# Moving a head's 512 negated maxima through a row in memory instead of eight transfers of 128

## The chip, the cores and the metric

The kernel runs on one core of one Trainium2 chip. The metric is the device time of one execution in microseconds (us). Before the change the median of three runs is 3677.85 us (3670.58, 3677.85 and 3678.45).

## The reference

A "macaron" layer on 4096 tokens of width 256 in float32: half a feed-forward layer, attention, half a feed-forward layer again, each behind a layer norm.

```python
x = x + 0.5 * ffn(layernorm(x))
x = x + attn(layernorm(x))
x = x + 0.5 * ffn(layernorm(x))
# attn: 16 heads of 16 channels
ctx = X @ We.T                                    # 32 channels
influence = einsum('bqe,bke->bqk', ctx, ctx)      # the same for all heads
scores = einsum('bhqd,bhkd->bhqk', Q, K) / 4 + 0.1 * influence[:, None]
attn = softmax(scores); out = (attn @ V) merged @ Wo.T
# ffn: both operands of each product are rounded to 4-bit floats in blocks of 16
```

The change lies in the attention: every query of every head needs the maximum of its 4096 scores, negated, before the exponentials.

## The kernel before, in words

**Stages.** A weights phase, a first feed-forward phase, a projection phase (q, k, v and ctx, parked in DRAM scratch), the attention, an output phase, and a second feed-forward phase. The attention takes 64 steps (STEPS). A step handles two heads (HEADS) and one block of 512 queries (QB, eight blocks to a pair of heads) against all 4096 keys.

**Two passes over the scores.** A coarse product (L1360) multiplies 128 queries by 512 keys into one of three PSUM banks, and VectorE (L1537) reduces the bank to its maximum per query in `tops`. A step has 64 such units, 32 to a head. They run ahead: in step s the coarse units 16 to 63 belong to step s+1, and units 0 to 15 to step s+2. After unit 32 VectorE folds head 0's 32 partial maxima into `neg_max` (L1551, 128 partitions x 4 columns: query j*128+p lies on partition p in column j); after the first unit of step s+2 it does so for head 1. The fine product (L1394) computes the scores transposed, 128 keys by 512 queries, in several accumulating products. ScalarE takes the exponential (L1522) into a ring of probabilities, and TensorE multiplies them by the values (L1404) into `o_ps`. A step has eight groups (NG); a group has eight coarse units, eight fine tiles and their products with the values, in an order written out by hand (SEGMENTS).

**How the maximum enters.** `queries.low[head][n]` holds, in each half of the partitions (rows r*64 on), the 32 rows of low parts of the queries, then at row 32 (M_ROW) the 512 negated maxima, then 16 more rows. The keys hold ones in that row, so the fine product subtracts the maximum. Both halves need the same row. Head 0's tile enters fine products named "low", and negated by GpSimd (`negate`, L1242) "old"; head 1's enters "new" (in the trace `fine<-area,key_d`). The tiles are double buffered over steps.

**SyncE's queue in step s.** SyncE issues nearly all transfers, in program order: wait until step s-1's exponentials are done (L1298); `load_low` for s+1, 8 transfers (L807, L809); `load_cross`, 2 (L801); `load_coarse` for s+2, 8 (L794, L795); `load_max(s+1, 0)`, 8 (L1280); then for the results of step s-1 `copy_sum` (2, L1125), `save_inverse` (1 to DRAM, L1130), `spread_inverse` (2 back, L1136) and `store` (2, L1143); in five of eight steps two transfers of the next pair's keys (L1263, L1265, L1272); last `load_max(s+1, 1)`, 8 (L1280).

**Who waits for what.** GpSimd, in order: `add_halves` for step s-1, `negate(s+1)` (needs head 0's maxima loaded, L1240), `multiply` for step s-1 (needs `spread_inverse`). VectorE inverts the sums at unit 50 (`INVERT_AFTER`, L1155), for which `copy_sum` must have landed. TensorE waits for `m_loaded` of head 0 and of head 1 only in group 0 of the step that uses them (L1457, L1462). Before it writes `neg_max[n]` again, two steps later, VectorE waits that the transfers that read it have ended (L1550).

Of the kernel before, what the change touches and what calls it, by code (L numbers as in the profile page):

```python
# [23 lines left out]
F32 = mybir.dt.float32  # L24
# [6 lines left out]
P = 128  # L31
T = 4096
TT = T // P
D = 256
# [3 lines left out]
DE = D // 8  # L38
# [5 lines left out]
QB = 512  # L44
NQB = T // QB
KT = T // P
QT = QB // P
KB = T // 512
HEADS = 2
STEPS = H // HEADS * NQB  # L50
# [703 lines left out]
HALF = P // 2  # L754


def half_rows(r, first, count):

    return slice(r * HALF + first, r * HALF + first + count)
# [339 lines left out]
M_ROW = 2 * DK  # L1099
# [63 lines left out]
def attention_phase(nc, sem, ident, v_all, scratch, sums, first_keys, probs, reload, first, area, second_low, parts, w):  # L1163

    with ExitStack() as ctx:
# [4 lines left out]
        queries = first.queries  # L1170
        tops = [sb(f"tops{n}", [P, HEADS * QT, KB]) for n in range(2)]
        neg_max = [sb(f"neg_max{n}", [P, HEADS * QT], F32R) for n in range(2)]
# [17 lines left out]
        k_loaded, low_keys_loaded = [[sem(f"{name}_loaded{n}") for n in range(2)] for name in ("k", "low_keys")]  # L1190
        m_loaded = [[sem(f"m_loaded{head}_{n}") for n in range(2)] for head in range(HEADS)]
        late_v, late_copied, part_ready = sem("late_v"), sem("late_copied"), sem("part_ready")
        table_loaded, negated = sem("table_loaded"), sem("negated")
        fine_ready, probs_ready, pv_done = sem("fine_ready"), sem("probs_ready"), sem("pv_done")
        coarse_ready, tops_ready, neg_ready = sem("coarse_ready"), sem("tops_ready"), sem("neg_ready")

        TILES = 2 * HEADS * PAIRS
        P_LEAD, V_LEAD = 2 * TILES_IN_GROUP, 4
        C_DMAS, K_DMAS, LOW_KEYS_DMAS, M_DMAS = [16 * 4, 16 * 2], 16 * 2, 16 * 8, 16 * 2 * QT
        LATE = KEPT * QT // 2  # L1200
        LATE_BLOCKS = sorted(range(NQB - KEPT, NQB), key=lambda b: b % KEPT < IN_AT)
        V_AFTER = [2 * i + 1 for i in range(LATE)]
# [21 lines left out]
        with nc.Block() as block:  # L1224
# [32 lines left out]
            def _(sp):  # L1257
# [16 lines left out]
                def load_max(s, head):  # L1274
                    n = s % 2
                    sp.wait_ge(neg_ready, HEADS * s + head + 1)
                    with nc.allow_non_contiguous_dma(reason="the maxima lie one to a partition"):
                        for r in range(2):
                            for j in range(QT):
                                sp.dma_start(queries.low[head][n][half_rows(r, M_ROW, 1), j * P:(j + 1) * P].bitcast(F32),  # L1280
                                             neg_max[n][:, head * QT + j:head * QT + j + 1].bitcast(F32)).then_inc(m_loaded[head][n], 16)

                for j in range(PIECES - 2, PIECES):
                    for r in range(2):
# [8 lines left out]
                for head in range(HEADS):  # L1293
                    load_max(0, head)

                def step(s):
# [10 lines left out]
                    if s + 1 < STEPS:  # L1307
                        load_max(s + 1, 0)
# [16 lines left out]
                    if s + 1 < STEPS:  # L1325
                        load_max(s + 1, 1)
# [337 lines left out]
def macaron_kernel(nc, x, wq, wk, wv, wo, we, w_gate, w_up, w_down, out):  # L1664
    with ExitStack() as ctx:
        sem = lambda name: ctx.enter_context(nc.semaphore(name))

        def sbufs(stack, shapes):
# [4 lines left out]
        ATTN_W = {f"{n}_{part}": ([P, KD, P if n == "e" else D], F32R) for n in "vqke" for part in ("hi", "lo")}  # L1673
        dram = {name: nc.dram_tensor("saved_" + name, shape, F32, kind="Internal").ap() for name, (shape, dt) in {**FFN_W, **OUT_W}.items()}
        scratch = {name: nc.dram_tensor("scratch_" + name, [rows, T], F32, kind="Internal").ap()
                   for name, rows in [("c_key", 2 * DE), ("c_query", 2 * DE)]} | {n: nc.dram_tensor("scratch_" + n, [D, 2, T], F32, kind="Internal").ap() for n in "qk"} | {"inv_sums": nc.dram_tensor("scratch_inv_sums", [STEPS, HEADS * QB], F32, kind="Internal").ap()}

        keep = sbufs(ctx, {"x_all": ([P, TT, D], F32), "ident": ([P, P], F32), "stats": ([P, TT, 6], F32),
                           "mean": ([P, TT], F32), "var": ([P, TT], F32), "tmp": ([P, TT], F32), "rstd": ([P, TT], F32), "root": ([P, TT], F32)})
# [23 lines left out]
        queries = Queries(sem, early_sb["slots"], [area[:, cols] for cols in SLOTS_IN_AREA], scratch)  # L1703
# [19 lines left out]
        second_low = both.enter_context(nc.sbuf_tensor("key_d0", [P, T // 2], F32R))  # L1723
        parts = [second_low[:, n * KD * QB:(n + 1) * KD * QB].rearrange("p (k t) -> p k t", k=KD) for n in range(2)]
        attention_phase(nc, sem, ident, v_all, scratch, sums, first_keys, probs, reload, first, area, second_low, parts, w)
        again.update({n: home[:, 0:KD * 2 * I].rearrange("p (a b) -> p a b", a=KD) for n, home in (("gu_hi", early_sb["slots"]), ("gu_lo", area))})
        output_phase(nc, sem, x_again, norm, again, parts, (o_reload, 16 * len(OUT_W)), (x_reload, 16 * X_PARTS), sums, [(again[n].bitcast(F32), dram[n], ffn_reload) for n in ("gu_hi", "gu_lo")])
# [20 lines left out]
```

## Time and profile before

| | us |
|---|---|
| median of three runs | 3677.85 |
| the profiled execution, its own time | 3675.19 |
| its span, first to last instruction | 3673.2 |
| PE busy | 3600.8 (98%) |
| DVE busy | 3165.5 (86%) |
| ACT busy | 2539.0 (69%) |
| POOL busy | 704.3 (19%) |
| DMA packets | 282101, 148.61 MB |

PE is TensorE's matmuls, PEld its weight loads, DVE VectorE, ACT ScalarE, POOL GpSimd, and SPq is SyncE's queue, where a row's duration is the time that issuing the transfer took. "Landing" is counted from the start of the issue. Times in a timeline are microseconds from the start of the span. Matmuls overlap in the pipeline, so a busy PE says little by itself: its waits are to be read at the weight loads, where an idle time stands in brackets with what ended it.

### The profile page before, as it was taken

How to read it: one execution, taken by the hardware profiler on the slowest of the kernel's cores; microseconds unless marked ns; L12 is line 12 of the kernel's file. 1: busy time of each engine (PE TensorE's matmuls, PEld its weight loads, DVE VectorE, ACT ScalarE, POOL GpSimd, SP SyncE). 2: the span in 40 equal slices, each digit the busy share in tenths (PEclk: the TensorE clock that was granted, in tenths of full speed). 3: DMA queues.
4: the chain of work that ended last, by engine and by line, in shares of the span. 5: the costliest groups of instructions: out<-in, count | busy, mean ns of one | idle time of the engine just before them, and what ended most of it. 6: DMA issues, size and time to landing. Idle time of an engine off the chain costs nothing. (4 is left out here: it accounts for less than half of the span.)

```text
span 3673.2 us, 71176 instructions
## 1 busy us (share of the span) xinstructions
PE 3600.8 (98%) x26663; PEld 2107.7 (57%) x26663; DVE 3165.5 (86%) x5176; ACT 2539.0 (69%) x4751; POOL 704.3 (19%) x509
## 2 busy tenths in 40 slices
PE   5998999999999999999999999999999999999999
PEld 4997655555555555555555555555555555554898
DVE  7996788888888888888888888888888888883898
ACT  4764277777777777777777777777777777777565
POOL 5991100000000000000000000000000000001697
PEclk9999999999999999999999999999999999999999
DMA  3003512111111111111111111111111111121100
GB/s 136 19 19 139 145 31 42 31 28 33 38 32 27 35 35 34 27 36 36 33 27 35 37 33 27 36 36 33 27 35 36 33 27 36 42 54 30 38 20 22
DMA packets 282101, 148.61 MB, mean 40 GB/s; under 512 B 181792, under 2 KB 233408, under 8 KB 280768
## 3 DMA queue, kind: packets, MB, share of 16 engines
q1 hardware_dynamic: 276976, 140.37, 16.1%
q10 hardware_dynamic: 4816, 4.10, 0.4%
q8 instruction: 197, 3.23, 0.4%
q14 instruction: 112, 0.92, 0.1%
HBM read 106.79 MB, written 32.51 MB: 38 GB/s over the span
## 5 line engine op out<-in xcount | busy, mean ns | idle before, releaser
L1537 DVE TENSOR_REDUCE tops<-coarse 128x1 f32<-128x512 f32 x4016 | 2547.0, 683 | 329.3 <-PE coarse L1360 273.6
L1522 ACT ACTIVATE x_all<-fine 128x512 f32<-128x512 f32 x4096 | 2115.0, 602 | 815.6 <-PE fine L1394 815.6
L1360 PE MATMUL coarse<-key_a,slots 48*128 48x512 f32 x4076 | 1292.1, 446 | 1.7 <-DVE tops L1542 1.2
L1404 PE MATMUL o_ps<-x_all,values 128*17 128x512 f32 x8192 | 1077.7, 598 | 0.6 <-ACT x_all L1522 0.6
L1360 PEld LDWEIGHTS coarse<-key_a,slots 48*128 48x128 f32 x4076 | 531.6, 184 | 909.9 <-DVE tops L1537 693.8
L1394 PE MATMUL fine<-slots,key_b 33*128 33x512 f32 (+1 forms) x3072 | 675.9, 394 | 0.0
L1394 PE MATMUL fine<-slots,key_a 48*128 48x512 f32 x2048 | 573.5, 420 | 0.0
L1394 PE MATMUL fine<-area,key_d 49*128 49x512 f32 x2048 | 563.6, 393 | 0.0
L1394 PE MATMUL fine<-slots,area 64*128 64x512 f32 x2048 | 409.1, 394 | 0.0
L1394 PEld LDWEIGHTS fine<-area,key_d 49*128 49x128 f32 x2048 | 368.3, 186 | 53.5
L1394 PEld LDWEIGHTS fine<-slots,key_b 33*128 33x128 f32 (+1 forms) x3072 | 340.6, 187 | 51.2 <-ACT x_all L1522 2.3
L1404 PEld LDWEIGHTS o_ps<-x_all,values 128*17 128x17 f32 x8192 | 135.8, 95 | 320.1 <-ACT x_all L1522 309.1
L1148 POOL COPY half<-ot 49x512 f32<-49x512 f32 x63 | 38.4, 609 | 1357.2 <-ACT ot L1483 1357.2
L1394 PE MATMUL fine<-area,key_b 49*128 49x512 f32 x1024 | 266.0, 395 | 0.0
L1394 PEld LDWEIGHTS fine<-slots,key_a 48*128 48x128 f32 x2048 | 246.6, 186 | 31.8 <-ACT x_all L1522 8.3
L1394 PEld LDWEIGHTS fine<-slots,area 64*128 64x128 f32 x2048 | 197.1, 186 | 42.5
L1160 POOL TENSOR_TENSOR wide<-total,wide 48x512 f32<-48x512 f32 x63 | 80.7, 1281 | 604.6 <-DMA wide<-scratch_inv_sums 604.6
L453 POOL TENSOR_TENSOR xn<-xn,step 128x960 f32<-128x960 f32 (+2 forms) x70 | 143.5, 2050 | 50.3 <-ACT step L619 49.4
L1394 PEld LDWEIGHTS fine<-area,key_b 49*128 49x128 f32 x1024 | 142.2, 186 | 14.9 <-ACT x_all L1522 9.2
L454 POOL TENSOR_TENSOR xn<-xn,step 128x960 f32<-128x960 f32 (+2 forms) x70 | 143.2, 2045 | 5.5
L631 ACT ACTIVATE sg<-g_ps 128x704 f32<-128x704 f32 x64 | 48.7, 761 | 126.5 <-PE g_ps L112 126.5
L459 POOL TENSOR_TENSOR dst<-xn,scale 128x960 f32<-128x960 f32 (+2 forms) x70 | 116.0, 1657 | 12.0 <-POOL xn L454 10.0
(232 smaller groups left out, 3177.7 us busy)
## 6 DMA issues: line engine op xcount, KB each, us to landing
slots<-scratch_c_query SPq DMA_DIRECT2D x256, 64.0 KB, 2.0
slots<-scratch_c_query SPq DMA_DIRECT2D x124, 128.0 KB, 2.9
slots<-scratch_q SPq DMA_DIRECT2D x384, 32.0 KB, 1.9
slots<-scratch_q SPq DMA_DIRECT2D x128, 64.0 KB, 1.9
area<-scratch_q SPq DMA_DIRECT2D x128, 64.0 KB, 2.0
slots<-neg_max SPq DMA_DIRECT2D x512, 0.5 KB, 2.0
area<-neg_max SPq DMA_DIRECT2D x512, 0.5 KB, 2.0
x_all<-in_L_attn_X SPq DMA_DIRECT2D x4, 1024.0 KB, 12.4
```

The source lines that it names most:

```text
L453: chain(pool.tensor_tensor(xn[n][:, cols], xn[n][:, cols], step[n][:, cols], ALU.add))
L454: chain(pool.tensor_tensor(xn[n][:, cols], xn[n][:, cols], step[n][:, cols], ALU.subtract))
L459: pool.tensor_tensor(blocks_of(dst[n][:, cols]), blocks_of(xn[n][:, cols]), spread(scale[n][:, lo:hi], hi - lo), ALU.mult).then_inc(q_read ...
L631: act.activation(sg[:, :], g_ps[:, 0:I], ACT.Silu).then_inc(sg_ready, 1)
L1148: eng.tensor_copy(self.half[:, :], self.ot[2 * 32:2 * 32 + self.BOTH, :]).then_inc(self.moved, 1)
L1160: eng.tensor_tensor(self.wide[:, :], self.total[0:32 + DK, :], self.wide[:, :], ALU.mult).then_inc(self.result_ready, 1)
L1360: return pe.matmul(bank, queries.coarse[head][t % queries.COARSE[head]][rows, q * P:(q + 1) * P], key_a[t // NQB % 2][rows, kb * 512:(kb + ...
L1394: return pe.matmul(fine[slot % 2][:, r, :], keys, query, start=what == "keys", stop=what in ("low", "new"), skip_group_check=what in PARTS[1])
L1404: last = pe.matmul(o_ps[32 * part:32 * part + DK + 1, :], v_all[:, head_of(s, head), kt, :], probs[:, ring(g, HEADS * head + which), r, :] ...
L1522: act.activation(probs[:, ring(g, slot), r, :], fine[slot % 2][:, r, :], ACT.Exp).then_inc(probs_ready, 1)
L1537: dve.tensor_reduce(tops[t % 2][:, head * QT + q, idx % KB:idx % KB + 1], coarse_bank(t, idx), AX.X, ALU.max).then_inc(tops_ready, 1)
```

## The change

The eight transfers of a head (two halves by four columns, each 128 elements of 4 B from 128 partitions to a part of a row) are replaced by one transfer of all 512 elements to a row of a new DRAM scratch tensor, in the order of the queries, a wait of SyncE for its landing, and one transfer from that row to both row halves. `m_loaded` now counts one transfer to a head.

```diff
-        table_loaded, negated = sem("table_loaded"), sem("negated")
+        table_loaded, negated, max_saved = sem("table_loaded"), sem("negated"), sem("max_saved")
...
-        C_DMAS, K_DMAS, LOW_KEYS_DMAS, M_DMAS = [16 * 4, 16 * 2], 16 * 2, 16 * 8, 16 * 2 * QT
+        C_DMAS, K_DMAS, LOW_KEYS_DMAS, M_DMAS = [16 * 4, 16 * 2], 16 * 2, 16 * 8, 16
...
                 def load_max(s, head):
                     n = s % 2
                     sp.wait_ge(neg_ready, HEADS * s + head + 1)
+                    row = scratch["maxima"][HEADS * n + head:HEADS * n + head + 1, :]
                     with nc.allow_non_contiguous_dma(reason="the maxima lie one to a partition"):
-                        for r in range(2):
-                            for j in range(QT):
-                                sp.dma_start(queries.low[head][n][half_rows(r, M_ROW, 1), j * P:(j + 1) * P].bitcast(F32),
-                                             neg_max[n][:, head * QT + j:head * QT + j + 1].bitcast(F32)).then_inc(m_loaded[head][n], 16)
+                        sp.dma_start(row.rearrange("a (j p) -> p (a j)", p=P), neg_max[n][:, head * QT:(head + 1) * QT].bitcast(F32)).then_inc(max_saved, 16)
+                    sp.wait_ge(max_saved, 16 * (HEADS * s + head + 1))
+                    sp.dma_start(queries.low[head][n][M_ROW:P:HALF, :].bitcast(F32), row.to_broadcast([2, QB])).then_inc(m_loaded[head][n], 16)
...
-                   ... | {"inv_sums": nc.dram_tensor("scratch_inv_sums", [STEPS, HEADS * QB], F32, kind="Internal").ap()}
+                   ... | {"inv_sums": nc.dram_tensor("scratch_inv_sums", [STEPS, HEADS * QB], F32, kind="Internal").ap(), "maxima": nc.dram_tensor("scratch_maxima", [2 * HEADS, QB], F32, kind="Internal").ap()}
```

## Rows read from the trace of the kernel before

**Rows 1.** Busy time by stretch: start:end, length, PE, PEld, DVE, ACT, POOL, PEclk, DMA, GB/s
```profile
452.00:3398.00 2946.00, 2944.59 (x22491) 1526.97 (x22492) 2562.82 (x4210) 2151.10 (x4166) 242.52 (x254) 1.00 0.16 34
```
**Rows 2.** Waits of PEld and DVE, 460 to 3390: us in total, times, longest
```profile
PEld coarse L1360 <- DVE tops L1537: 692.3, 814, 0.9
PEld o_ps L1404 <- ACT x_all L1522: 308.8, 994, 1.5
...
DVE few L1155 <- DMA few<-total: 19.5, 1, 19.5
```
**Rows 3.** Busy time by group of one step, columns as in rows 1
```profile
1654.15:1659.90 5.75, 5.75 (x46) 2.98 (x46) 5.06 (x9) 4.63 (x10) 1.88 (x2) 1.00 0.41 103
1659.90:1665.65 5.75, 5.75 (x46) 3.00 (x46) 5.15 (x10) 4.13 (x9) 0.00 (x0) 1.00 0.08 1
1688.65:1694.40 5.75, 5.75 (x46) 2.98 (x46) 5.08 (x9) 4.15 (x9) 0.00 (x0) 1.00 0.03 0
```
**Rows 4.** Timeline of ACT, the first exponentials of successive groups
```profile
1660.94 2.07 ACT L1522 ACTIVATE x_all<-fine 128x512 f32<-128x512 f32 x4 [0.93 <-PE fine L1394]
1666.68 2.07 ACT L1522 ACTIVATE x_all<-fine 128x512 f32<-128x512 f32 x4 [0.92 <-PE fine L1394]
...
1689.75 2.06 ACT L1522 ACTIVATE x_all<-fine 128x512 f32<-128x512 f32 x4 [0.91 <-PE fine L1394]
1695.49 2.06 ACT L1522 ACTIVATE x_all<-fine 128x512 f32<-128x512 f32 x4 [0.92 <-PE fine L1394]
```
**Rows 5.** Timeline of SyncE's queue in the same step: start, duration
```profile
1660.98 5.03 SPq L1280 DMA_DIRECT2D slots<-neg_max  x8
1666.05 1.23 SPq L1125 DMA_DIRECT2D few<-total  x2
1674.27 0.31 SPq L1130 DMA_DIRECT2D scratch_inv_sums<-few  x1
1675.65 0.77 SPq L1136 DMA_DIRECT2D wide<-scratch_inv_sums  x2
...
1684.06 5.81 SPq L1280 DMA_DIRECT2D area<-neg_max  x8
1694.59 0.31 SPq L807 DMA_DIRECT2D slots<-scratch_q  x1
```
**Rows 6.** Timeline of DVE in it
```profile
1673.92 0.33 DVE L1155 RECIPROCAL few<-few 32x32 f32<-32x32 f32 x1
```
**Rows 7.** Timeline of POOL in it
```profile
1667.58 0.62 POOL L1242 TENSOR_SCALAR area<-slots 113x512 fp32r<-113x512 f32 x1 [10.79 <-DMA slots<-neg_max]
```
**Rows 8.** Timeline of PE, the next step's first product with head 1's maxima
```profile
1697.83 0.62 PE L1394 MATMUL fine<-area,key_d 49*128 49x512 f32 x2
```
**Rows 9.** DMA issues: count, KB each, median us from issue to landing
```profile
slots<-neg_max SPq DMA_DIRECT2D x512, 0.5 KB, 2.0
...
wide<-scratch_inv_sums SPq DMA_DIRECT2D x128, 32.0 KB, 1.8
...
few<-total SPq DMA_DIRECT2D x128, 2.0 KB, 1.8
...
scratch_inv_sums<-few SPq DMA_DIRECT2D x64, 4.0 KB, 1.3
```
**Rows 10.** Tile key_d, 1640 to 1702: one issue's ns min/median/max, then landing
```profile
L1265 SPq DMA_DIRECT2D key_d<-scratch_k x2: 590/608/626, 1680.4 to 1681.0; - x2
...
DMA to landing us min/median/max: 3.9/4.1/4.4
```
**Rows 11.** Queue of the transfers, 1660.9 to 1666.2: packets, MB, share of 16 engines
```profile
q1 hardware_dynamic: 1008, 0.00, 10.2%
```
**Rows 12.** Timeline of POOL: one row to a step
```profile
1240.54 0.61 POOL L1148 COPY half<-ot 49x512 f32<-49x512 f32 x1 [21.68 <-ACT ot L1483]
...
1470.58 0.61 POOL L1148 COPY half<-ot 49x512 f32<-49x512 f32 x1 [21.70 <-ACT ot L1483]
...
1931.27 0.61 POOL L1148 COPY half<-ot 49x512 f32<-49x512 f32 x1 [21.75 <-ACT ot L1483]
```

More of the change, by code:

```diff
@@ L1675, in macaron_kernel @@
         scratch = {name: nc.dram_tensor("scratch_" + name, [rows, T], F32, kind="Internal").ap()
-                   for name, rows in [("c_key", 2 * DE), ("c_query", 2 * DE)]} | {n: nc.dram_tensor("scratch_" + n, [D, 2, T], F32, kind="Internal").ap() for n in "qk"} | {"inv_sums": nc.dram_tensor("scratch_inv_sums", [STEPS, HEADS * QB], F32, kind="Internal").ap()}
+                   for name, rows in [("c_key", 2 * DE), ("c_query", 2 * DE)]} | {n: nc.dram_tensor("scratch_" + n, [D, 2, T], F32, kind="Internal").ap() for n in "qk"} | {"inv_sums": nc.dram_tensor("scratch_inv_sums", [STEPS, HEADS * QB], F32, kind="Internal").ap(), "maxima": nc.dram_tensor("scratch_maxima", [2 * HEADS, QB], F32, kind="Internal").ap()}
         keep = sbufs(ctx, {"x_all": ([P, TT, D], F32), "ident": ([P, P], F32), "stats": ([P, TT, 6], F32),
```

## The prediction

> **What bounds the kernel now.** I read the busy times by stretch first. The attention, 452 to 3398 us, is 80% of the span; TensorE always has something in its pipeline there, at a granted clock of 1.00, and the DMA engines are 16% busy [rows 1]. A busy PE hides waits, so the waits come next, taken at the weight loads: 692.3 us until VectorE has reduced a coarse bank and 308.8 us until ScalarE has made probabilities [rows 2]. The stage is a ring of three engines. No wait of TensorE on a transfer is on that list. VectorE waited for one once, 19.5 us in the last step, where it has no coarse work left; no maxima are loaded in that step.
>
> The question is then whether the maxima's transfers touch the ring at all. The views by group say they do not. Three groups of one step have 5.75 us each, by the shares of PE and by the starts of ScalarE: the one in which the query loads run (DMA share 0.41), the one in which head 0's eight transfers run (0.08), and the last of the step, in which nearly nothing moves (0.03) [rows 3]. ScalarE's first exponentials of successive groups are 5.74 us apart over head 0's transfers (1660.94 to 1666.68) and 5.74 us apart over the quiet group (1689.75 to 1695.49) [rows 4]. The reader is to see that eight issues, 1024 small packets and SyncE busy for 5 us leave no mark on the pace, to 0.01 us.
>
> **What the change removes.** Per head and step, eight issues of 0.60 us and a little between them: 5.03 us for head 0, and 5.81 us in this step for head 1 [rows 5]; 64 steps of two heads make 1024 transfers and 131072 of the page's 282101 packets. The last of eight is issued 7/8 into that stretch (4.4 us) and lands 2.0 us after its issue [rows 9]: the maxima are home 6.4 us after SyncE starts. That agrees with GpSimd, which waits for head 0's and starts at 1667.58, 6.60 us after 1660.98 [rows 7].
>
> **What it adds.** One store of 512 pieces of 4 B to memory, a wait, and one load of two rows of 2 KB.
> - Issue. The trace has no store of 512 pieces, but it has loads of 512 (32 rows by 16 blocks of 512 B): 0.61 us to issue [rows 10]. Ends: 0.31 us, the store of the inverted sums [rows 5], and 4 times 0.60 = 2.4 us, if an issue went with its number of elements. I take 0.6; the landing counts from the start of the issue, so only the 2.4 matters, for the upper end.
> - The store's landing. Ends: 1.3 us, the only kind of small store to memory in this stage (32 pieces of 128 B, [rows 9]), and 4.4 us, the slowest transfer of 512 pieces in its window, with 128 times the bytes [rows 10]; adding the 1.8 us by which the issue may be longer, 6.2. Between them: 1008 packets, nearly all of them these 4 B ones, took 10.2% of 16 engines over 5.3 us, which is 8.7 us or 8.6 ns a packet [rows 11]. Spread over 16 engines 512 of them add 0.3 us; one after another they would add 4.4, for 5.7. I take 1.3 + 0.3, rounded up to 2.0 because it is nearest to today's transfers of the same pieces, which land in 2.0 [rows 9].
> - The wait. SyncE's next issue followed the landing of the inverted sums by 0.1 us (1674.27 + 1.3 to 1675.65) [rows 5, 9].
> - The load: 1.8 us, as the spread of the inverted sums, a row from memory to many partitions [rows 9].
>
> Sum: 2.0 + 0.1 + 1.8 = 3.9 us to the landing, in place of 6.4; ends 1.3 + 0.1 + 1.8 = 3.2 and 6.2 + 0.1 + 1.8 = 8.1 us. SyncE is held for 2.0 + 0.1 + about 0.6 = 2.7 us instead of 5.03. So the maxima are most likely earlier by 2.5 us, and at the worst of these bounds later by 1.7 us.
>
> One rule of the Trainium skill speaks against the change. "DMA: Bandwidth & Descriptors", Anatomy of one DMA, puts most of a transfer's fixed 2 us into the receipt from the target memory and calls HBM the heaviest target; its Specifications add that pieces under 512 B are read, modified and written. The trace has it the other way round for the receipt: the store to memory is the quickest to land, 1.3 us, against 2.0 into SBUF [rows 9]. By the page's about 2 us for the store the sum on the path would be 0 as well. What its read-modify-write could do to 512 neighbouring 4 B pieces no row here shows, and it is the second rival below.
>
> **Who is late then.** Four parties use what this touches, and I take the margin of each in this step.
> 1. VectorE's inversion at unit 50, at 1673.92 [rows 6], behind `copy_sum`, which is queued behind the new wait. After the store's landing come 0.1 us, the load's issue 0.65, the first of two issues 0.65, and 1.8 to the landing of the second [rows 9]: 3.2 us. So the store may take 1673.92 - 3.2 - 1660.98 = 9.7 us before VectorE waits. It takes 2.0 (6.2 at the upper bound). VectorE's place does not move forward with it: it is in the order of its own queue. So the whole chain behind it (save, spread, GpSimd's multiply, store, SyncE's next loads) starts at 1674.27 as now.
> 2. GpSimd's negation, at 1667.58 now [rows 7], which only the next step needs: its exponentials begin at 1695.49, 28 us on [rows 4].
> 3. TensorE's first product with head 1's maxima, at 1697.83 [rows 8], behind a start at 1684.06: room 13.8 us, used 3.9 (8.1 at most).
> 4. SyncE itself: next wanted at 1694.59 [rows 5], free at 1684.06 + 2.7 instead of at 1689.87. What it issues there waits for ScalarE, not for SyncE. The same holds in the three of eight steps without key loads, and in those with them, of which this is one.
>
> The start (maxima of step 0) has the same form, with its consumers over 10 us behind, and the last maxima are loaded a whole step before the end. VectorE's own wait before it writes `neg_max` again is two steps old. So the sum on the path is 64 x (0 + 0) = **0 us**, hidden by the ring's own pace in every term. If the cover were gone, the price would be 1 us a step for each us over 9.7.
>
> The profiled execution took 3675.19 us, 1.99 over its span, and the sum leaves it there; the median of the runs is 2.66 us above it (0.07%), within their spread of 7.9. I forecast **3676.5**, between the two. One thing may move although nothing waits: the ring runs at two paces. From 1240.54 to 1470.58 a step takes 46.01 us, from there to 1931.27 it takes 46.07 [rows 12]. Other timing on SyncE could tip the mix; all 64 steps at one pace or the other are 4 us apart, and the trace's mix lies between, so this is worth -3 to +2 us. With the runs' spread around the profiled one (-4.6 to +3.3) the likeliest case's own range is 3669 to 3682.
>
> **Rivals.**
> - *Faster: the packets and issues saved act on the ring after all*, because the engines' own reads and writes meet fewer small pieces. For it: 65,000 of 282,101 packets go. Against it: the groups of equal length [rows 3, 4]. To count for more than 0.2% it needs 7.4 / 128 = 0.06 us for each group with maxima, six times the 0.01 us that those groups leave. Time if it were 0.08: 128 x 0.08 = 10 us less, 3665.
> - *Slower: the store's 4 B pieces are taken by the memory one after another.* It decides where the store takes over 9.7 us, in every step, at VectorE's inversion. At the 8.6 ns of a packet the serial store takes 5.7 us and stays hidden. At twice that, 17.2 ns, it is 1.3 + 8.8 = 10.1 us, 0.4 over: 62 x 0.4 = 25 us, 3700. At three times, 14.5 us, it is 62 x 4.8 = 298 us, 3973. For it: no row shows so small a piece going to memory. Against it: 32 pieces of 128 B there are the quickest landing in the table.
> - *The change doesn't do what it says*: the one transfer to both halves is cut into 4 B pieces as well, 1024 of them. Landing of some 2.0 to 6.2 us, still inside the room of head 1 (6.2 + 0.1 + 6.2 = 12.5 of 13.8). The time is the forecast's, 3676.5.
>
> **How the numbers follow.** Two executions of this kernel can't be told apart below about 0.2%, 7.4 us. The likeliest case, hidden in full, has 0.86 (with the third rival's 0.02 inside it); the faster rival 0.06; the slower one 0.06; 0.02 stay for a change of pace or drift beyond the spread, half to each side. Hence faster 0.07, same 0.86, slower 0.07. The range is the likeliest case's, which holds 8 in 10, stretched at the upper end to 3685 for a store just past its margin and at the lower to 3668.
>
> **What would show it.** In the profile after: some 216,000 packets; 128 stores landing in 1.5 to 3 us and 128 loads in about 1.8; SyncE's `few<-total` some 2 us earlier against the neg_max before it, and the inversion still in VectorE's order with no new idle time before it; no `maxima` among the waits of PEld or DVE; steps of 46.0 to 46.1 us. Wrong would be: `DVE few <- DMA` with tens of us, a store landing over 9.7 us, or groups with maxima shorter than the others.

## The result and the profile after

The changed kernel takes 3706.55 us (median of four runs, 3704.61 to 3712.66), the kernel before beside it 3675.76 (3670.58 to 3678.45): a ratio of 1.0091, interval 1.0078 to 1.0103. It is slower by 0.9%, where no change was forecast, and lies 21.5 us above the end of the range. The profiled execution took 3706.20 us with a span of 3704.1, 30.9 us more span than before.

The stage first: attention, in the columns of [rows 1], over the stretch in which it runs now.

```profile
452.00:3428.00 2976.00, 2956.57 (x22488) 1527.05 (x22485) 2566.07 (x4209) 2154.23 (x4166) 242.08 (x254) 1.00 0.15 34
```

VectorE and ScalarE are busy for the same time as in [rows 1] within 3.3 us each, and the stretch is 30 us longer: it is idle time. PE, which was idle for 1.4 us of it, is idle for 19.4. The waits of PEld and DVE over 460 to 3420 (us in total, times, longest) answer to [rows 2]:

```profile
PEld coarse L1360 <- DVE tops L1537: 719.4, 844, 2.0
PEld o_ps L1404 <- ACT x_all L1522: 297.4, 956, 1.5
...
DVE few L1155 <- DMA few<-total: 41.2, 27, 21.0
```

The last line is the new one. Of its 27 waits one is the last step's, 21.0 us (19.5 before). The other 26, with 20.2 us, are new: VectorE waits for `copy_sum` in 26 steps. TensorE's waits for VectorE grow by 27 us, and their longest is 2.0 us where it was 0.9: the stall is passed on.

What `copy_sum` waits for is SyncE, and SyncE waits for the store. This is its whole new wait (us, times, longest), and below it SyncE's queue in the step of [rows 5]:

```profile
SPq L1281 <- DMA scratch_maxima<-neg_max: 1104.0, 123, 11.1
```

```profile
1676.45 0.38 SPq L1279 DMA_DIRECT2D scratch_maxima<-neg_max  x1
1687.35 0.50 SPq L1281 DMA_DIRECT2D slots<-scratch_maxima  x1
1687.89 1.40 SPq L1125 DMA_DIRECT2D few<-total  x2
1691.36 0.31 SPq L1130 DMA_DIRECT2D scratch_inv_sums<-few  x1
```

The store is issued in 0.38 us and the load behind it starts 10.90 us after it. Over all steps that distance has a median of 9.18 us for head 0 (8.54 to 11.43) and 9.08 for head 1 (7.15 to 11.5). Before, the eight issues held SyncE for 5.03. On VectorE the inversion, with no bracket in [rows 6], now has one (idle time, and what ended it):

```profile
1688.79 0.69 DVE L1537 TENSOR_REDUCE tops<-coarse 128x1 f32<-128x512 f32 x1 [0.36 <-PE coarse L1360]
1690.99 0.34 DVE L1155 RECIPROCAL few<-few 32x32 f32<-32x32 f32 x1 [1.51 <-DMA few<-total]
```

GpSimd's copy, one to a step, gives the steps as in [rows 12]. This step and the one before it:

```profile
1624.18 0.61 POOL L1148 COPY half<-ot 49x512 f32<-49x512 f32 x1 [21.59 <-ACT ot L1483]
...
1670.29 0.61 POOL L1148 COPY half<-ot 49x512 f32<-49x512 f32 x1 [21.64 <-ACT ot L1483]
...
1717.97 0.61 POOL L1148 COPY half<-ot 49x512 f32<-49x512 f32 x1 [21.75 <-ACT ot L1483]
```

The first is 46.11 us long, the second, with the wait of 1.51, 47.68. So by these marks the 30.9 us lie as follows: 27.6 in 61 steps of the middle (46.495 on average against 46.042), of which the 26 steps with an inversion wait hold 25.7 and the rest 1.9; 1.0 up to the first mark, where PE waits 0.5 us for head 1's maxima; 1.4 in the last step, where PE waits once for head 1's maxima (1.2 us); 0.9 behind it.

The queue says what kind of time the store's is. Above, the 3 us from 1676.4, with the store; below, the 7 us from 1655 in the step before, in which head 1's store, issued at 1653.44, has not landed yet (the load behind it starts at 1662.42):

```profile
q1 hardware_dynamic: 528, 0.00, 8.5%
```

```profile
DMA packets 0, 0.00 MB, mean 0 GB/s; under 512 B 0, under 2 KB 0, under 8 KB 0
```

The 528 packets are recorded together, in 3 x 16 x 0.085 = 4.1 us of engine time or 7.7 ns each; the last ends at 1677.73, 1.3 us after the start of the issue. Then nothing is recorded, for some 9.6 us, until the store reports. The packets' own time, which [rows 11] gave as 8.6 ns, is not where the store's time goes.

### The profile page after: what moved, and what is told of

It reads as the page before. It is cut to its first block and busy times, and to the rows that moved or that the text cites. A ratio compares the mean times of both kernels' runs of the same rounds, so it can differ in the third digit from the quotient of the medians.

```text
span 3704.1 us, 70408 instructions
## 1 busy us (share of the span) xinstructions
PE 3614.3 (98%) x26663; PEld 2109.2 (57%) x26663; DVE 3170.2 (86%) x5176; ACT 2542.1 (69%) x4751; POOL 703.5 (19%) x509
## 2 busy tenths in 40 slices
DMA packets 202735, 148.77 MB, mean 40 GB/s; under 512 B 102176, under 2 KB 153792, under 8 KB 201408
## 5 line engine op out<-in xcount | busy, mean ns | idle before, releaser
L1360 PE MATMUL coarse<-key_a,slots 48*128 48x512 f32 x4076 | 1292.9, 447 | 16.5 <-DVE tops L1537 15.1
L1242 POOL TENSOR_SCALAR area<-slots 113x512 fp32r<-113x512 f32 x32 | 19.7, 617 | 552.0 <-DMA slots<-scratch_maxima 552.0
## 6 DMA issues: line engine op xcount, KB each, us to landing
x_all<-in_L_attn_X SPq DMA_DIRECT2D x4, 1024.0 KB, 12.4
```

The costliest lines, as they stand in the source:

```text
L1360: return pe.matmul(bank, queries.coarse[head][t % queries.COARSE[head]][rows, q * P:(q + 1) * P], key_a[t // NQB % 2][rows, kb * 512:(kb + ...
```

## The experiments

Theory: the store of 512 neighbouring words lands in 9 to 10 us, and `copy_sum`, queued behind SyncE's wait, reaches VectorE's inversion late. What had to be told apart: whether that order is the whole loss, why the store is slow, and what each us over the margin costs.

**1. The sums ahead of the maxima** (on the changed kernel; `copy_sum` is no longer behind the store's wait).

```diff
+                    if s > 0:
+                        sums.copy_sum(sp, s - 1)
                     if s + 1 < STEPS:
                         load_max(s + 1, 0)
                     if s > 0:
-                        sums.copy_sum(sp, s - 1)
                         sums.save_inverse(sp, s - 1)
```

> The changed kernel with the copy of the sums issued ahead of head 0's maxima instead of behind them. Theory (the stores take about 9.2 us and VectorE's inversion waits for the copy queued behind them): the idle time of VectorE before the inversion falls from 41 us to the last step's 20, the stores still take 9 us, the average step falls from 46.49 to about 46.1, and the time to 3675 to 3685 us; what is left above the kernel before is head 1's store, where it passes 13.8 us with its load. Rival (the transfers through memory slow the engines or the memory directly, the place in the queue does not matter): 3700 to 3710 us, steps of 46.5.

Measured: 3690.27 us (3687.40 to 3693.05), ratio 1.0044 (1.0028 to 1.0061), between the theory's range and the rival's. The inversion waits in the last step alone, and the store is as slow as before (median 9.6 for head 0):

```profile
DVE few L1155 <- DMA few<-total: 21.3, 1, 21.3
...
SPq L1281 <- DMA scratch_maxima<-neg_max: 1053.2, 112, 11.5
...
PE fine L1395 <- DMA area<-scratch_maxima: 4.8, 5, 2.3
```

So the queue's order explains about half of the loss (3706.55 to 3690.27). What is left of it, 17 us against the kernel before, is not at the inversion. In the span it is 3.2 us before the attention begins, where the change has done nothing yet; 4.4 up to the first step's mark, where the fine products wait 2.3 us for head 1's maxima and TensorE then runs 461 to 467 at a granted clock of 0.50; 7.4 in 61 steps; and 1.7 in the last (0.3 come back behind it). The third row above shows a part of these stalls: TensorE waits for head 1's maxima in the first step, in the last (1.6 us) and in three between (0.15 to 0.5), behind stores of 9.4 to 11.4 us. It also stands still for 1.4 us at 1520.8 and for 1.2 at 1568.4, just as head 1's two stores of 11.7 us end. There it waits for ScalarE and not for the maxima, and around 1520 VectorE and ScalarE are idle for over 2 us as well. What holds all three there isn't shown.

**2. Stores of other shapes** (on the kernel before, which still does all its work). In each step, behind `copy_sum`, SyncE issues one store, waits for it, and issues a mark; eight forms take turns, so each has seven or eight measurements. The distance from store to mark is the landing plus about 0.02 us (from the last update of the store's semaphore to the next issue).

```diff
+                    sp.dma_start(dst, src).then_inc(probed, 16)          # one of eight forms
+                    sp.wait_ge(probed, counted)
+                    sp.dma_start(scratch["mark"]..., ident[0:32, 0:32]).then_inc(probed, 16)
```

> The kernel before, with one extra transfer and its wait in SyncE's quiet stretch of each step, behind the copy of the sums, and a small marking store behind the wait; its form goes by the step modulo 8. Read is the time from its issue to the mark. Forms of 0 to 7: 512 pieces of 4 B to memory as in the change; 128; 256; 512 pieces 64 B apart; 512 pieces 1 KB apart; 512 pieces of 4 B inside SBUF; 128 pieces of 16 B to memory; 496 pieces on 124 partitions. Theory A (each of 16 engines waits for the memory piece by piece): 9 us for form 0, 3 for 128, 5 for 256, the spacing changes nothing, form 7 takes several times as long if its pieces go on fewer engines. Theory B (neighbouring pieces meet in one memory line that is read, changed and written): 64 B apart falls to 2 to 3 us. Theory C (512 pieces cost this wherever they go): form 5 takes 9 us too. By A and B it takes 2 to 2.5.

> As the other probe, with other forms, 0 to 7: 128 pieces of 4 B on 32 partitions; 1024 pieces of 4 B; 512 pieces of 32 B; of 64 B; 512 pieces of 4 B read from memory into SBUF; 512 pieces of 4 B, 16 B apart; 16 pieces of 128 B; 512 pieces of 512 B, all to memory but the read. Theory A (piece by piece, whatever the size): 1024 pieces take 17 us, 32 B and 64 B as long as 4 B, 9 us. Theory B (pieces smaller than a line are read, changed and written): 64 B fall to 2 to 3 us and 512 B to 3 to 4, 1024 take 17. The read takes 2 to 3 us in both.

> The third probe on the kernel before. Forms 0 to 7, pieces of 4 B to memory if nothing else is said: 128, 16 adjacent, such groups 1 KB apart; 128 adjacent, neighbours by different engines; 128, 8 adjacent, groups 1 KB apart; 512, 32 B apart; 512, 8 B apart; 512 pieces of 8 B; 512 pieces of 16 B; 128, 64 B apart. Theory L (writes to the same 64 B line follow each other): 8 us for the first and second form, 4 to 5 for the third, 2 to 2.5 for 32 B apart, 5 for 8 B apart and for 8 B pieces, 3 to 4 for 16 B pieces, 2 for 64 B apart. Theory R (writes to the same 512 B region follow each other): the first and third form fall to 2 to 3 us, the second stays at 8, 512 of 8 B or 8 B apart take 5, 16 B pieces 3.

Medians in us, range in brackets. P is 128 partitions; "words" are pieces of 4 B to memory unless said otherwise.

| form | store to mark |
|---|---|
| 512 words next to each other, as in the change | 9.72 (9.38-12.22) |
| 256 / 128 words next to each other | 9.00 / 8.30 |
| 1024 words next to each other | 10.34 |
| 128 next to each other, each word's neighbour from 8 partitions away | 7.42 |
| 512 next to each other, 124 partitions | 7.11 |
| 128 words in four runs of 32, runs 512 B apart | 3.95 (3.76-5.57) |
| 128 words in eight runs of 16, runs 1 KB apart | 2.21 (1.87-2.65) |
| 128 words in runs of 8, runs 1 KB apart | 2.02 |
| 512 words, 8 B / 16 B apart | 4.04 / 3.91 |
| 512 words, 32 B / 64 B / 1 KB apart | 2.10 / 2.05 / 2.05 |
| 512 pieces next to each other, of 8 B / 16 B | 4.32 / 2.92 |
| 512 pieces next to each other, of 32 B / 64 B / 512 B | 1.98 / 1.99 / 2.52 |
| 128 pieces of 16 B next to each other / 16 of 128 B | 2.2 / 1.59 |
| 128 words 64 B apart | 1.67 |
| 512 words inside SBUF / read from memory | 2.07 / 2.48 |

SyncE's queue in the first probed kernel: 512 words next to each other, then 128, then 512 words 64 B apart, then 512 pieces inside SBUF.

```profile
1575.24 0.58 SPq L1311 DMA_DIRECT2D scratch_probe<-ident  x1
...
1585.42 0.31 SPq L1314 DMA_DIRECT2D scratch_mark<-ident  x1
...
1621.84 0.58 SPq L1311 DMA_DIRECT2D scratch_probe<-ident  x1
...
1629.77 0.31 SPq L1314 DMA_DIRECT2D scratch_mark<-ident  x1
...
1713.00 0.58 SPq L1311 DMA_DIRECT2D scratch_probe<-ident  x1
...
1715.05 0.31 SPq L1314 DMA_DIRECT2D scratch_mark<-ident  x1
...
1805.53 0.69 SPq L1311 DMA_DIRECT2D probe_sb<-ident  x1
...
1807.59 0.31 SPq L1314 DMA_DIRECT2D scratch_mark<-ident  x1
```

10.18, 7.93, 2.05 and 2.06 us. So the expectations' theory C (512 pieces cost this wherever they go) falls with the store inside SBUF, and theory A (piece by piece, whatever the spacing and size) with the spaced words. Neither the size of a piece nor the number of them is slow: 512 words are as quick as anything when they lie 32 B apart or more. They are slow when they are neighbours in memory. The number of neighbours matters, and hardly the total: 128 words in one run take 8.3, the same 128 in four runs of 32 take 3.95, in runs of 16 take 2.21; and from 128 to 512, one run being four times as long, it adds only 1.4. That reads as stretches of memory that work side by side, each taking its pieces one after another; this picture is inferred. By an estimate from the table, about 0.1 us a piece and a stretch of about 256 B fit most rows (64 pieces: 8.3 to 9.7; 32: 3.9 to 4.3; 8: 2.0). They don't fit all: 16 pieces in such a stretch take 2.2 in one form and 3.9 in another (16 B apart), and 124 partitions instead of 128 save 2.6. A stretch of 64 B doesn't explain that 16 words in it are quick, nor one of 128 B that a run of 128 costs twice what a run of 32 does. Theories L (64 B) and R (512 B) both miss rows. One rival is untested: what counts may be how many DMA engines write into a stretch, and not only how many words lie in it. The semaphore of the store from 124 partitions is counted up in 5 updates and that of the runs of 16 in 9, the other forms' in up to 16; if every engine that takes part reports once, these two use fewer engines, and the first of them is quicker than 512 words for it. So the size of the stretch and what goes on in it stay open. That the nearness of the words in memory is the cause doesn't.

**3. The row's words 64 B apart** (on the changed kernel: same transfers, same wait, same order; only the scratch row is 16 times as long, so that the load reads single words too).

```diff
-                    row = scratch["maxima"][HEADS * n + head:HEADS * n + head + 1, :]
+                    row = scratch["maxima"][HEADS * n + head:HEADS * n + head + 1, :].rearrange("a (q e) -> a q e", e=16)[:, :, 0]
...
-                   ... "maxima": nc.dram_tensor("scratch_maxima", [2 * HEADS, QB], ...)
+                   ... "maxima": nc.dram_tensor("scratch_maxima", [2 * HEADS, QB * 16], ...)
```

> The changed kernel with the words of the row 64 B apart in memory; the number of pieces, the queue, the wait and the places are the same, only the load now reads words too. Theory (4 B pieces that share a line of memory are written one behind another): the store lands in about 2.05 us, VectorE's idle time before the inversion falls to the last step's 20 us, steps of 46.05 us, 3670 to 3680 us. Rival (a transfer to memory and a wait in this queue cost it, whatever the spacing): 3700 us and more.

Measured: 3675.62 us (3672.48 to 3677.51, ten runs) against 3675.94 for the kernel before: ratio 1.0 (0.999 to 1.0009). The whole loss is gone with the spacing alone. SyncE's queue in one step, and VectorE's inversion in it, without a bracket again:

```profile
1613.22 0.38 SPq L1279 DMA_DIRECT2D scratch_maxima<-neg_max  x1
1615.28 0.54 SPq L1282 DMA_DIRECT2D slots<-scratch_maxima  x1
1615.87 4.75 SPq L1125 DMA_DIRECT2D few<-total  x2
```

```profile
1626.16 0.33 DVE L1155 RECIPROCAL few<-few 32x32 f32<-32x32 f32 x1
```

The store's wait is 2.06 us, and the steps are back at 46.04 us. The third row is a price that stays covered: the load now reads 1024 words, lands in 4.8 us at the median, and the two issues of `copy_sum` behind it take 4.75 us instead of 1.23.

**4. Pieces of 16 B** (on the changed kernel: query 4p+j on partition p, so that the four maxima of a partition are neighbours; the coarse product takes every fourth query as its weights, and the results are the same).

```diff
-                        sp.dma_start(row.rearrange("a (j p) -> p (a j)", p=P), ...
+                        sp.dma_start(row.rearrange("a (p j) -> p (a j)", p=P), ...
...
-                    return pe.matmul(bank, queries.coarse[...][rows, q * P:(q + 1) * P],
+                    return pe.matmul(bank, queries.coarse[...][rows, q:QB:QT],
```

> The changed kernel with query 4p+j on partition p and column j (TensorE reads every fourth query as a coarse product's weights), so that the store writes 16 B pieces in a row, 128 of them, and the load reads the row as it is. Theory: the store lands in 1.7 to 3.3 us as the probe's, nothing waits, 3670 to 3680 us. Rival (weights read at a stride of 16 B load more slowly, or sharing a line is as bad at 16 B as at 4 B): weight loads above 184 ns, or stores of 9 us and 3700 us.

Measured: 3857.16 us, ratio 1.0491 (1.0474 to 1.0509); the rival with the slower weight loads came. The store became quick, and the weights slow. First SyncE's queue, then the weight loads of the coarse product (ns min/median/max), this kernel's row and, in the next fence, that of the kernel before over 500 to 3300 us:

```profile
1617.48 0.34 SPq L1279 DMA_DIRECT2D scratch_maxima<-neg_max  x1
1618.91 0.50 SPq L1281 DMA_DIRECT2D area<-scratch_maxima  x1
```

```profile
L1360 PEld LDWEIGHTS coarse<-key_a,slots x4076: 303/306/333, 397.1 to 3520.4; 64*128 64x128 f32 x98, 48*128 48x128 f32 x97
```

```profile
L1360 PEld LDWEIGHTS coarse<-key_a,slots x3893: 182/183/188, 500.2 to 3300.0; 64*128 64x128 f32 x98, 48*128 48x128 f32 x97
```

The store lands in 1.4 us, but 64 coarse units a step load weights at a stride of 16 B in 306 ns instead of 183. The step is 48.88 us long, 2.8 more; 64 times 0.12 are 7.9, so most of the longer loads is hidden. The store's own part can't be read from the total.

**5. The slow store beside the kernel before** (the same 512 neighbouring words twice a step, never waited for except ahead of the next such store).

```diff
+                def beside(s, at):
+                    sp.wait_ge(probed, 16 * (2 * (s - 1) + at))
+                    sp.dma_start(scratch["beside"][at:at + 1, :].rearrange("a (j p) -> p (a j)", p=P), ident[:, 0:QT]).then_inc(probed, 16)
```

> The kernel before, unchanged on its path, with the slow store (512 words next to each other in memory) issued beside it twice a step, at the places where the changed kernel has it, and waited for only before the next one. Theory (the cost is in the waits behind the store): 3672 to 3682 us, steps of 46.0 to 46.1. Rival (a store in progress also delays others, above all the fetch of instructions, which took 1.8 instead of 1.2 us a packet in the changed kernel): 3685 to 3695 us, with gaps of 1 to 2 us on all engines at once.

Measured: 3686.51 us (3684.73 to 3697.14), ratio 1.0033 (1.0021 to 1.0044), 10.6 us more, with no wait of the kernel on that store; the rival's range holds it. So it disturbs others. One place where it shows: SyncE's queue, and TensorE in the next step.

```profile
3029.44 5.04 SPq L1281 DMA_DIRECT2D area<-neg_max  x8
3034.52 0.59 SPq L1300 DMA_DIRECT2D scratch_beside<-ident  x1
```

```profile
3043.00 0.40 PE L1404 MATMUL fine<-slots,key_b 49*128 49x512 f32 x2
...
3046.12 0.76 PE L1404 MATMUL fine<-area,key_d 49*128 49x512 f32 x1 [2.73 <-DMA area<-neg_max]
```

```profile
3047.00:3050.00 3.00, 3.00 (x16) 0.60 (x14) 1.34 (x2) 1.99 (x4) 0.00 (x0) 0.50 0.88 169
```

Head 1's eight transfers are all issued by 3034.5, and such ones land in 2.0 us [rows 9]; TensorE gets the last of them only at about 3046, some 12 us after its issue. The semaphore that counts them says the same: 127 of its 128 updates are there by 3035.86, and the last comes at 3045.99, among the sixteen of the slow store (3042.35 to 3046.16). After the idle 2.73 us the granted clock is 0.50 (the lower of TensorE's two levels, 1.2 GHz) for 3 us. The step is 4.5 us longer, of 15.1 us in 61 steps; one more step with a stretch at 0.50 holds 2.2. The queue of the instructions, 197 packets of 16 KB, suffers too: its share is 0.4% before and with the row spaced, and 0.6% here and in the changed kernel.

```profile
q8 instruction: 197, 3.23, 0.6%
```

In the changed kernel such a packet takes 1.69 us on average (1.16 before), and one in twenty over 3.8 (1.4 before). How much of the 10.6 us is late instructions and how much late data no run here tells.

**6. Time added to the chain.** First on the changed kernel: one more small store (32 pieces of 128 B), waited for, between head 0's store and its load.

```diff
+                    if head == 0:
+                        sp.dma_start(scratch["spare"]..., ident[0:HEADS * DK, 0:HEADS * DK]).then_inc(max_saved, 16)
+                        sp.wait_ge(max_saved, ...)
```

> The changed kernel with one small store (32 pieces of 128 B) and its landing put between head 0's store and its load, some 1.4 us more in SyncE's queue in every step. Theory (margin of 9.7 us, of which 9.2 are used, then 1 us a step for each us over it): the median head 0 now passes the margin by 0.9 us, 62 steps cost about 55 us more, 3755 to 3775 us, and VectorE's idle time before the inversion is 90 to 120 us. Rival (the cost is not in that wait): within 10 us of the changed kernel, 3706 us.

Measured: 3854.99 us, ratio 1.0497 (1.0472 to 1.0521), 80 us over the upper end expected. The small store is issued after the slow one has landed, and still it is slowed (us, times, longest), and the inversion waits in every step:

```profile
SPq L1284 <- DMA scratch_spare<-ident: 106.9, 64, 4.7
```

```profile
DVE few L1155 <- DMA few<-total: 145.4, 63, 20.8
```

From store to load it is 11.6 us at the median (14.84 at most). The small store itself takes over 1.6 us in 22 of 64 cases, up to 5.0 (in the kernel with seven of them below, 41 of 448, up to 3.5). In the 61 middle steps 122.1 us of waits stand against 168.7 us more time. Then four and seven such stores on the kernel of experiment 3, whose own store is quick, so that nothing slow is in memory:

```diff
+                    if head == 0:
+                        for i in range(4):                               # and 7
+                            sp.dma_start(scratch["spare"]..., ident[0:HEADS * DK, 0:HEADS * DK]).then_inc(max_saved, 16)
+                            sp.wait_ge(max_saved, ...)
```

> The version with the words 64 B apart, with four small stores (32 pieces of 128 B), each waited for, between head 0's store and its load. Nothing in it shares a region, so only the length of the chain counts. Theory (room of 9.7 us before VectorE waits): the chain takes 2.05 + 4 x 1.4 = 7.7 us, nothing waits, 3672 to 3682 us. Rival (every us in this chain costs, because SyncE is late with the rest): about 5.6 us a step, 4000 us.

> The same with seven small stores. Theory (9.7 us of room, then 1 to 1.35 us a step for each us over it, as the changed kernel's steps with a wait and those with the extra store show): the chain takes 2.05 + 7 x 1.4 = 11.9 us, 2.2 over, 62 steps: 136 to 184 us more, 3810 to 3860 us. Rival (the room is another, or the price is not linear in the excess): outside that.

Measured: 3747.76 us (3746.37 to 3751.28, ratio 1.0198) with four and 4122.11 (4119.92 to 4125.51, ratio 1.1212) with seven. Both miss, upwards. The kernel with four, SyncE and VectorE in one step:

```profile
1642.99 0.38 SPq L1279 DMA_DIRECT2D scratch_maxima<-neg_max  x1
1645.14 4.29 SPq L1283 DMA_DIRECT2D scratch_spare<-ident  x4
...
1650.99 0.54 SPq L1286 DMA_DIRECT2D slots<-scratch_maxima  x1
1651.58 4.02 SPq L1125 DMA_DIRECT2D few<-total  x2
```

```profile
1656.80 0.34 DVE L1155 RECIPROCAL few<-few 32x32 f32<-32x32 f32 x1 [0.78 <-DMA few<-total]
```

The expectations used 9.7 us of room. In these kernels it is less, because the issues of `copy_sum` behind the word-wise load take 4.02 us instead of 1.23: some 7 us. With seven stores the chain (head 0's store to its load) is 12.14 us on average and the wait 4.84; a straight line through the 62 steps gives a wait of 1.00 x chain - 7.3. So the wait is the chain less its room, us for us, and the room is 7.3 us. With four stores the chain is 7.9 on average and the wait 0.80. The step grows by more than the wait: 1.10 us for 0.80 (1.37) and 7.14 for 4.81 (1.48) on average over the 61 middle steps, 168.7 us for 122.1 (1.38) with the one small store, and in the changed kernel's 26 steps 25.7 for 20.2 (1.27). A part of the reason shows in the changed kernel around its longest stall (columns as in [rows 1]):

```profile
846.00:849.70 3.70, 3.70 (x32) 2.02 (x29) 2.48 (x4) 2.61 (x6) 0.62 (x1) 1.00 0.04 7
849.70:851.70 2.00, 0.48 (x5) 0.05 (x1) 0.94 (x3) 0.60 (x1) 0.00 (x0) 1.00 0.00 0
851.70:855.30 3.60, 3.60 (x15) 1.21 (x15) 2.43 (x4) 1.57 (x3) 0.56 (x1) 0.54 0.07 19
```

PE is busy for 0.48 of 2 us, and in the 3.6 us behind that its granted clock is 0.54: 15 matmuls there, where 32 fitted into 3.7 us ahead of the stall. This is the only one of the 26 stalls with such a stretch behind it: 3.4 us at 0.50, at half speed a loss of 1.7 us. The other 25 cost more than their length too, 1.2 times on average, and what makes the rest is open. With longer stalls the clock matters more: with the one small store the steps with a stretch at 0.50 behind the stall grow by 1.61 of their waits (21 steps) and the others by 1.09 (40), with four stores by 1.90 (9) and 1.10 (34), and with seven every step has such a stretch.

## Why the prediction was wrong

**The step that failed is the store's landing**, a term of the sum: taken as 2.0 us with ends 1.3 and 6.2, it measured 9.2 at the median and up to 11.4. With the load the sum came to 12.4 us instead of 3.9: the maxima are home 6 us later than before, not 2.5 earlier. The upper end was not an end. Its 4.4 us were those of a load of 512 pieces of 512 B into SBUF, which has neither the small pieces nor the target. The serial case beside it, 5.7 us, was made from packet times (8.6 ns, one after another), and the packets are over 1.3 us after the issue while the landing takes nine. And its other leg, the quick store of the inverted sums in [rows 9], has pieces of 128 B; no row had several small pieces in one stretch of memory, which is what experiments 2 and 3 show to matter. The value was taken from today's transfers of the same words because they were nearest; their target is SBUF, where 512 take 2.07 us. The nearest row had the right pieces and the wrong target.

**What came is close to the slower rival**: its place, VectorE's inversion, and its point, a store of over 9.7 us, are right, though it comes in 26 steps and not in every one. Its mechanism, all pieces one after another, is not: 128, 256, 512 and 1024 neighbouring words take 8.3, 9.0, 9.7 and 10.3 us, so the time hardly goes with the number. The rival was given 0.06, since it needed more than twice the time of a packet for each piece. Spacing the words, with the rest of the change in place, takes all of the loss away (experiment 3), so nothing else in the change costs anything that can be measured. The cause of the loss is shown by that; how the memory takes neighbouring words is only inferred.

**The rule weighed there.** The row on which the trace seemed to contradict the rule, 1.3 us for a store to memory, stands: stores whose pieces are 32 B or longer, or that far apart, land in 1.3 to 2.5 us. The Trainium skill, "DMA: Bandwidth & Descriptors", Specifications, has pieces under 512 B read, modified and written. Size alone doesn't bear on the time here: 512 words 64 B apart take 2.05 us and 512 pieces of 512 B take 2.52. Among neighbours a turn of read and write for each piece would look like what was measured, but no run here sees it happen. The section of the Trainium skill that the prediction names beside it, Anatomy of one DMA, describes transfers issued by GpSimd, while SyncE issues these. Its ranking of the targets isn't borne out here: memory is not the slower target for pieces that lie apart: 512 words 1 KB apart take 2.05 us and 512 inside SBUF 2.07.

**The other steps.**
- Issue 0.6 us: 0.38. The wait of 0.1: 0.02. The load, taken as 1.8: it lands in 3.2 us at the median by its semaphore (1.7 to 4.3), a second term that was too small.
- Margin 1, 9.7 us at the inversion, was read right, and used wrongly. It was compared with one value. The median of the stores, 9.2, is inside it, and still 26 steps wait: all of head 0's stores over 9.7 together exceed it by only 12.8 us, and the waits are 20.2. The rest comes from `copy_sum` itself, right behind the store and the load: its two issues take over 1.5 us in 15 steps (up to 3.4), where 6 did before (up to 2.4), and 19 of its landings take over 3 us (up to 4.6), where 4 did before (up to 3.5). Before, 5 us of slack covered them. With `copy_sum` ahead of the store (experiment 1) both are as rare as before, 2 and 3.
- Margin 2, GpSimd: right, no wait there. Margin 3, TensorE with head 1's maxima: right but for two waits, 0.5 us in the first step and 1.2 in the last; its 13.8 us of room are used by 12.3 at the medians, not by 3.9. With the order of experiment 1 it has five such waits.
- The price beyond the margin, 1 us for each us: 1.27 to 1.48. The late clock is 1.7 us of that in the changed kernel and most of it with four and seven stores.
- Costs nowhere in the sum: that the store holds up other transfers and the instructions while it lands, and some just after, 10.6 us when all its waits are taken away (experiment 5). This doesn't add to the 26 waits, as the late landings among them are part of it. What the share of each is in the 30.8 us isn't settled; experiment 1 and experiment 5 put the part that is not the queue's order between 10 and 17 us.
- Packets: 216,000 forecast, 202,735 on the page. A transfer has more of them than its pieces: the store 528 for 512, and the 1008 of [rows 11] are seven times 144 for 128. So a head's eight had 1152, not 1024.
- The third rival, a load cut into 1024 pieces: not so. In the 3.6 us behind a load, from 1687.3, there are 34 packets of 4 B.
- The faster rival: nothing of it was seen; the changed kernel's steps without a wait are no shorter than before. Experiment 3 speaks of it from the other side: with 768 transfers fewer but 333,551 packets instead of 282,101 the time is that of before within 0.1%.

The signs that the forecast named as "wrong" all came: `DVE few <- DMA` with 20 us beyond the last step's, and stores over 9.7 us.

## What to carry to other kernels

A transfer that gathers words from many partitions into neighbouring words of memory is the costly case: write the words 32 B or more apart, or in pieces of 32 B or more, or leave them in SBUF, and look at what a strided reader of that layout then pays. Take a landing from a landing of the same pieces into the same target and the same neighbourhood, never from packet times, and where no row has one, let the range say so. Compare a margin with the spread of what uses it, and remember that a change which leaves every engine's work alone can still spend the slack that covered their irregularities.

## What the runs showed of the hardware

- 512 neighbouring words take 9.7 us to memory and 2.05 us when 64 B apart; 128 neighbouring ones take 8.3, and 2.2 in eight runs of 16. The packets' recorded time is the same 8 ns either way.
- While such a store is landing, others land late, data and instructions: the last of eight transfers that land in 2.0 us took some 12, an instruction packet 1.69 us on average where it took 1.16. It does not end with the landing: a small store issued right after it took up to 5.0 us where 1.3 is usual.
- A load of 1024 words lands in 4.8 us, in time here, and makes the next two issues on its queue take 4 us together instead of 1.2.
- Weights of 4 B elements at a stride of 16 B load in 306 ns instead of 183.
- Behind 2.0 us in which PE was busy for 0.48 the granted clock was 0.54 over 3.6 us, and behind an idle 2.7 us it was 0.50 over 3 us. Stalls at the inversion cost 1.27 to 1.48 times their length on average, 1.1 to 1.2 times where the clock stayed up.
